# A graph network's tile loop in another order: four-batch tiles alternating with merged ones, SyncE's queue unrolled

## The reference, cut to what matters

```python
dst = (12500 * uniform(400000) ** 2).astype(int32); order = argsort(dst)
# layer 0: Gaussian mixture convolution, K = 3 kernels over edge attributes
gauss = exp(sum(-0.5 * (attr - mu)**2 / (eps + sigma**2)))
aggr  = segment_sum(einsum('eko,ek->eo', (x[src] @ g).reshape(E, 3, 64), gauss), dst) / max(cnt, 1)
x = layernorm(x + silu(aggr + x @ root_w + bias + x))
# layer 1: two mean-aggregating convolutions
h = relu(x @ W_self1 + (segment_sum(x[src], dst) / deg) @ W_neigh1 + b1)
x = layernorm(x + h @ W_self2 + (segment_sum(h[src], dst) / deg) @ W_neigh2 + b2)
```

## Time and profile before

| | us |
|---|---|
| median of 3 runs | 7653.07 |
| profiled execution | 7651.4 |
| its span | 7649.6 |
| TensorE busy | 5050.4 (66%) |
| VectorE busy | 4374.6 (57%) |
| GpSimd busy | 3367.5 (44%) |
| ScalarE busy | 2714.0 (35%) |

### The profile page before, as it was taken

How to read it: one execution, slowest core, us unless ns; L and a number is a source line. 1 busy time by engine, 2 the same in 40 slices (tenths; PEclk the granted TensorE clock), 3 DMA queues, 4 the chain that set the end, 5 groups by cost and what they waited for, 6 DMA issues and landing times.

```text
span 7649.6 us, 144672 instructions
## 1 busy us (share of the span) xinstructions
PE 5050.4 (66%) x35195; PEld 4048.2 (53%) x35196; DVE 4374.6 (57%) x15088; ACT 2714.0 (35%) x8317; POOL 3367.5 (44%) x3146
## 2 busy tenths in 40 slices
PE   1565655555566666655555555555545899999999
PEld 1223333333344444444444444444425899999999
DVE  5668888767677777665656656566543322222222
ACT  3113333334444444455555555555532000000000
POOL 5024555555666666666666666666630000000000
PEclk9558888877788888777778888788775899999999
DMA  2001222212222222222222222222230799999998
GB/s 71 28 24 49 68 68 68 67 51 87 78 96 83 87 91 90 90 90 91 90 90 91 91 90 90 73 90 90 91 85 3 298 381 383 381 367 385 385 384 344
DMA packets 258352, 1082.32 MB, mean 141 GB/s; under 512 B 140102, under 2 KB 144230, under 8 KB 194406
## 3 DMA queue, kind: packets, MB, share of 16 engines
q1 hardware_dynamic: 142806, 968.66, 32.8%
q0 software_dynamic: 100352, 102.96, 6.9%
q10 hardware_dynamic: 14902, 8.11, 0.5%
HBM read 751.67 MB, written 327.81 MB: 141 GB/s over the span
## 4 chain that ended last, share of the span: by engine, by line
PE 39%; DVE 20%; issue 14%; DVEq 13%; POOL 5%; DMA 5%; ACT 4%; ACTq 1%; SPq 1%; POOLq 0%
PE pw L970 21%; PE pw L800 9%; DVE rE L1269 5%; POOL rE L512 5%; DVEq L1302 3%; DMA tab<-tab_d 3%; DVEq L1472 3%; PE pw L825 3%; DVE rE L1267 2%; DVE rE L1329 2%; PE pw L772 2%; ACT rE L559 1%; DVE rE L1395 1%; PE pw L937 1%; ACT sca L575 1%
## 5 line engine op out<-in xcount | busy, mean ns | idle before, releaser
L512 POOL DMA_INDIRECT rE<-in_x,idx x3136 | 3365.4, 1073 | 2262.7 <-issue 2092.9
L800 PE MATMUL pw<-rE 128*128 128x193 f32 x7824 | 1775.9, 391 | 921.5 <-DVE rE L1329 885.9
L598 ACT CAST rB<-pw 128x792 bf16<-128x792 f32 x1568 | 1259.6, 814 | 2903.6 <-PE pw L825 1489.4
L800 PEld LDWEIGHTS pw<-rE 128*128 128x128 f32 x7824 | 1623.7, 233 | 1130.5 <-DVE rE L1329 1061.5
L559 ACT ACTIVATE rE<-rE,cols 128x64 f32<-128x64 f32 x4704 | 1254.5, 344 | 8.2 <-DMA tab<-tab_d 8.2
L825 PE MATMUL pw<-rE 128*128 128x396 f16 x3840 | 804.1, 357 | 577.8 <-DVE rE L1269 576.8
L1269 DVE TENSOR_SCALAR rE<-iperm,gr 128x392 f16<-128x392 f16 x3840 | 1052.1, 314 | 0.0
L825 PEld LDWEIGHTS pw<-rE 128*128 128x128 f16 x3840 | 368.8, 103 | 954.4 <-DVE rE L1269 681.1
L970 PE MATMUL pw<-rB,rA 128*128 128x192 bf16 x9604 | 810.8, 246 | 0.1
L970 PE MATMUL pw<-rE,rA 128*128 128x192 bf16 x9604 | 810.4, 246 | 0.1
L970 PEld LDWEIGHTS pw<-rB,rA 128*128 128x128 bf16 x9604 | 790.8, 98 | 1.6
(11 more groups left out here) (256 smaller groups left out, 2626.6 us busy)
## 6 DMA issues: line engine op xcount, KB each, us to landing
rA<-count SPq DMA_DIRECT2D x392, 1568.0 KB, 8.5
count<-rB SPq DMA_DIRECT2D x98, 3136.0 KB
rE<-in_x,idx POOLq DMA_INDIRECT x3136
cols<-cols_d SPq DMA_DIRECT2D x98, 64.0 KB
cols_d<-rA SPq DMA_DIRECT2D x3, 1568.0 KB, 5.2
rA<-in_edge_attr ACTq DMA_DIRECT2D x1, 4608.0 KB
out<-gcol ACTq DMA_DIRECT2D x97, 32.0 KB, 5.8
count<-rB SPq DMA_DIRECT2D x8, 224.0 KB, 2.0
```

The lines of the kernel that those rows point to most:

```text
L512: pool.indirect_dma_start(out=gath[:, s, u * CB + b, :], out_offset=None, in_=x, in_offset=bass.IndirectOffsetOnAxis(ap=idx[:, s, u * CB + ...
L598: act.copy(stage[:, s, :, j * 2 * W:(j + 1) * 2 * W].rearrange("p h (w n) -> p w h n", w=2), pu[j % 3][:, :, 0:CW].rearrange("p w (h n) -> ...
L800: ins = pe.matmul(sums[side][:, 0:AW], onehot[:, side, bb, :], wgath[:, side, bb, :], start=(bb == 0), stop=(bb == CB - 1))
```

## The change

Every engine goes through the tiles by position q instead of t. ORDER gives the tile of a position: 0, 1, 2; then 48, 3, 49, 4, ... 60, 15; then 61; then 16 to 47; then 62 to 97. NI = 13, QC = 30 is the first position of the two-batch tiles and QM = 62 that of the last merged ones. Semaphores count positions; which node tile is worked on, and which DRAM rows are read and written, comes from ORDER.

- TensorE, VectorE and ScalarE get a loop of 13 rounds whose body is a merged tile (always slot 1) followed by a four-batch tile (always slot 0).
- A four-batch tile now prepares the merge of the tile behind it. The merge works on a buffer of its own, `gm`.
- `merge_ahead` stands behind unit 6 instead of unit 4, and ScalarE's copies come one window later.
- A merged tile behind one of another kind (`behind=2`) waits for more used ring slots before its first units.
- SyncE's loops are written out: 98 times the same steps, with constant addresses, no registers.

```diff
+NI = T4 - DT - 1
+QC = DT + 2 + 2 * NI
+QM = QC + TM - T4
+ORDER = list(range(DT + 1)) + [t for i in range(NI) for t in (TM + i, DT + 1 + i)] + [TM + NI] \
+    + list(range(T4, TM)) + list(range(QM, 98))
...
+        gm = sb("gm", [P, LP])
...
-            for part, (base, n) in enumerate(PARTS):
-                end = part == len(PARTS) - 1
-                with sp.Fori(0, n // 2 - 2 * end, 1) as i:
-                    for s in range(2):
-                        after(part, i * 2 + s, s)
...
+            for q in range(NT):
+                part = max(k for k, (base, _) in enumerate(PARTS) if ORDER[q] >= base)
+                sp.wait_ge(a_evac, q * NU + (NU + 2))
+                sp.wait_ge(a_bnd, q + 1)
+                sp.dma_start(tile_of(count[part][0], ORDER[q] - PARTS[part][0]), stage[:, q % 2, None, 0:NT, :]).then_inc(a_st[q % 2], 16)
+                if q + 2 < NT:
+                    sp.wait_ge(a_list, q + 1)
+                    load_cols(q + 2)
+                if q + 3 < NT:
+                    for u in range(U):
+                        sp.wait_ge(a_g[1 - q % 2][u], 16 * CB * ((q + 1) // 2 + 1))
+                    load_idx(q + 3)
...
-                        if merged == "parts" and 6 <= j < 10:
-                            copied(i * 2 + (s + 1), 1 - s, j - 6)
+                        if merged == "parts" and 7 <= j < 11:
+                            copied(m, 1 - s, j - 7)
...
+            with act.Fori(0, NI, 1) as i:
+                windows(i + 1, 1)
+                windows(i + 2, 0, False, "parts", i + 1)
...
-                        dve.wait_ge(a_used, t * NU + (n + 1))
+                        free = n + 1 if behind < 2 else max(n + 1, min(n + 3, 4))
+                        dve.wait_ge(a_used, q * NU + free)
...
-                        if n == 4 and not last:
-                            merge_ahead(t + 1)
-                        if n == NU - 2 and not last:
-                            merge(t + 1)
...
+            def merge_between(n, q, following, other):
+                t, m = following
+                if n == 6:
+                    merge_ahead(q + 1, t, m, other)
+                if n == NU - 2:
+                    merge(m)
...
-            tile_counts(DT, 2, late=False)
-            with dve.Fori(0, T4 - DT - 1, 1) as i:
-                tile_counts(i + (DT + 1), 2)
...
+            tile_counts(DT, DT, 2, late=False, s=0, following=(TM, 0))
+            with dve.Fori(0, NI, 1) as i:
+                merged_counts(i * 2 + (DT + 1), i + TM, s=1)
+                tile_counts(i * 2 + (DT + 2), i + (DT + 1), 2, s=0, following=(i + (TM + 1), i + 1))
+            merged_counts(QC - 1, TM + NI, s=1)
+            with dve.Fori(0, QM - QC, 1) as i:
+                tile_counts(i + QC, i + T4, 1)
```

More of the change, by code:

```diff
@@ L384, in _ @@
             sp.sem_inc(a_col, 1)
-            for s in range(2):
-                load_cols(s, s)
+            for q in range(2):
+                load_cols(q)
             for u in range(U):
                 sp.wait_ge(a_g[0][u], 16 * CB)
[L389 to L409, removed]
+            load_idx(2)
             def tile_of(c, t):
@@ L574, in copied, with windows @@
                                             skip_runtime_bounds_check_because="the tables hold places of two columns")
-                    ins = act.copy(both[:, :, j], gr[:, bass.ds(at, 2)])
+                    ins = act.copy(both[:, :, j], gm[:, bass.ds(at, 2)])
                 if part is None or part == 3:
                     ins.then_inc(a_mrg, 1)
-            def windows(i, s, last, merged=None):
+            def windows(i, s, last=False, merged=None, m=None):
                 act.wait_ge(a_st[s], 16 * i + 1)
@@ L860, in listed, with tile_counts @@
                 pe.sem_inc(a_list, 1)
-            def tile_counts(t, pairs_w, late=True):
-                s = pe.snap(t % 2, min_val=0, max_val=1) if not isinstance(t, int) else t % 2
+            def tile_counts(t, pairs_w, late=True, s=None):
+                other = next_of(t) if s is None else 1 - s
+                s = pe.snap(t % 2, min_val=0, max_val=1) if s is None else s
                 for u in range(U):
@@ L871, in tile_counts @@
                         if late and n == 2 // max(1, pairs_w) - 1:
-                            listed(next_of(t) if not isinstance(t, int) else 1 - t % 2)
+                            listed(other)
                         if n % (NU // U) == 1:
@@ L1481, in tile_counts @@
                         if late and n == 2 // pairs_w - 1:
-                            listed(t - 1, slot_of(t + 1) if not isinstance(t, int) else 1 - t % 2)
-                            base_of(t)
+                            listed(q - 1, other)
+                            base_of(q, t)
                         if n % (NU // U) == 1:
-                            prepare(t, s, u)
+                            prepare(q, s, u)
+                        if following is not None:
+                            merge_between(n, q, following, other)
                 for k in range(2):
@@ L1495, in _ @@
             dve.sem_inc(a_pair, DT * NU)
-            tile_counts(DT, 2, late=False)
-            with dve.Fori(0, T4 - DT - 1, 1) as i:
-                tile_counts(i + (DT + 1), 2)
-            dve.wait_ge(a_used, T4 * NU + RU)
-            for _ in range(22):
-                dve.sem_inc(s_tick[3], 1)
-            with dve.Fori(0, TM - T4, 1) as i:
-                tile_counts(i + T4, 1)
-            dve.wait_ge(a_pair, TM * NU)
-            merge_ahead(TM)
-            merge(TM)
-            for _ in range(1):
-                dve.sem_inc(s_tick[3], 1)
-            with dve.Fori(0, NT - 1 - TM, 1) as i:
-                merged_counts(i + TM)
-            merged_counts(NT - 1, True)
+            tile_counts(DT, DT, 2, late=False, s=0, following=(TM, 0))
[5 more added lines that the diff above has]
+                tile_counts(i + QC, i + T4, 1)
+            dve.wait_ge(a_pair, QM * NU)
+            merge_ahead(QM, QM, QM - TM, 0)
+            merge(QM - TM)
+            with dve.Fori(0, NT - 1 - QM, 1) as i:
+                merged_counts(i + QM, i + QM, behind=1, following=(i + (QM + 1), i + (QM + 1 - TM)))
+            merged_counts(NT - 1, NT - 1, s=1, behind=1)
             listed(NT - 1, (NT - 1) % 2)
```

141 lines of the change are left out of this document (75 added, 66 removed).

## The result

| | us, median (lowest to highest), runs |
|---|---|
| before, beside the changed kernel | 7653.09, 4 runs |
| after | 7416.6 (7410.16 to 7425.55), 4 runs |
| ratio, 95% interval | 0.9692 (0.9675 to 0.9708) |
| profiled execution after | 7417.34, span 7415.5 |

The forecast was 7560 (7500 to 7635).

The account below looks back on a forecast made before the run. VectorE was taken to set the pace up to tile 48, GpSimd's gathers after that. Terms -72 (pairs), -15 (lead) and -5 (last tiles) sum to -92: 7651.4 to 7559, median 1.7 higher, 7560 us; range 7500 to 7635.

Parts of the forecast that it names:

- The pair: Alternating four-batch and merged tiles: VectorE's sum of 115.3 less 5.0 gives about 110 us a pair, -72 in all.
- each kind had both before: nothing: Table load L1302 at tile starts: fixing merged tiles to slot 1 and four-batch ones to slot 0 costs 0.
- The block repeats its 1640.9: Two-batch tiles 16 to 47 follow with buffers full as before, take 1640.9 us again, so 0 saved.
- the longest that two buffers allow: Lead (start of a tile's L1415 minus start of its first gather) at tile 16: 121 us, taken as the maximum.
- The -15 for the lead: Tile 62 begins with a lead of 39 us, not 24, so the last gather comes 15 us earlier.
- The -5 for merge_ahead: Merged tiles 62 to 97: later merge_ahead gives nothing while gathers bound; 5 of 12 us of tab waits go at the end.
- Gathers bound the pair: Rival, chance 0.08: in the alternating tiles the pair falls to 98 us, set by gathers; kernel 7410 us.
- The waits change hands: Rival, chance 0.08: vanished tab waits in merged tiles return as waits for TensorE and ScalarE; 7655 us, no change.
- Slower by instruction fetch: Rival, chance 0.10: VectorE's longer pair loop pays a fetch of 9.4 us per pair; kernel 7682 us.
- ScalarE's copies in four-batch tiles: 32 copies of 0.19 us a tile, covered by ScalarE's waits for TensorE: taken as 0, 51 us if uncovered.
- the stricter wait on the ring: First merged window pairs: VectorE waits for the last four-batch unit; taken as 0, bounded by 25 us in all.
- SyncE's queue: Unrolled queue sheds register work ahead of its issues: taken as 0, at best 5 us of the last tiles' tab waits.

Follow-up runs that it names:

- the order alone: Changed kernel with merge_ahead back behind window pair 4 and 64 increments ahead of VectorE's two-batch loop: 7514.96 us, ratio 0.9819.
- The two single edits: Changed kernel with merge_ahead and ScalarE's copies back early: 7473.82 us, ratio 0.9767; kernel before with both late: 7597.89 us, ratio 0.9932.

## Why the forecast was wrong

The forecast counted nearly all of its gain as one cause, the order, and gave the place of merge_ahead 5 us. There were three causes, and they add: 7652 - 7515 = 137 us for the order, 50 for the place of the two-batch loop, 57 for the place of merge_ahead (each of the last two alone; both together 7515 - 7417 = 98).

*The pair (term mis-sized, -72 forecast, -137 measured).* Mechanism and bound were right: a pair costs VectorE's sum, no DMA wait in it, ScalarE never short of gathers, GpSimd stalling. The pair took 104.7 us and not 110. VectorE's busy time is the same, 55.4 + 29.1 = 84.5 us in a four-batch tile and one of tiles 48 to 52 before, 1096.6 / 13 = 84.4 in a pair. So all is in the gaps, 11.7 + 18.6 = 30.3 before and 20.3 after. I took 5.0 off, and listed only the waits of the merged tiles for it: that is the step that failed. The largest wait stood in the other tile: 69.2 us by issue ahead of L1346, 5.3 a four-batch tile, of which 2.0 / 13 = 0.2 is left, now that this tile follows in straight code. (That straight code is the reason was tested only at the other head, where it took 2.0 of 7.0 away.) Against it stand 7.0 us a pair at the loop's new head (25.8 + 64.3 over 13) where a merged tile had 3.9 (19.5 in tiles 48 to 52), so 2.1 net. Part of that is a zero of the forecast that was none. The table load takes 4.7 us from slot 1 and 1.6 from slot 0, and "each kind had both before: nothing" overlooks that only the merged tile's load is still waited for, and that it now always comes from slot 1 (64.3 / 13 = 4.9 us a pair). With merged tiles in slot 0 it would be some 3.1 us a pair less, 40 in all; this is an estimate, no run tried it. The others, per pair: the table's DMA 4.5 (I had 3.5), the list's waits 4.6 to 3.2, and L1367 1.0, which I had at 0.6. L1249 did not fall, 4.8 to 5.1, where I had 0.9. These five give 8.7 of the 10.0. Neither constant slots nor the place of merge_ahead change the pair: 104.2 and 104.8 us with those taken back.

*"The block repeats its 1640.9" (step failed).* With the order alone it does, 1641.7, and tile 62 begins with a lead of 36 us, forecast 39. The step failed because it took the block's code to stay as it was. I had the fetch as a rival for the new loop and looked for it as a cost that the change adds. It was a cost that the old kernel paid, 3.0 us at each jump of the two-batch loop, and that the new program's length happened to remove. The rows named for it were those of the four-batch loop; the issue time of the two-batch loop (200.1 us) and the queue's 268 packets stood in the same trace and were not used. The lead at the start of the block was not the same either, 81 us and not 121: "the longest that two buffers allow" is no fixed number. GpSimd may start a tile some 12 us behind the mark two tiles back (above), so the longest lead is two tiles of that stage less 12.

The Trainium skill (Runtime: NRT & Kernel Launch, Instruction fetch mechanics) says that instructions stand in two 16 KiB pages and that a taken branch out of them stalls. The four packet counts and the 3.0 us above agree with such a stall. Which loop pays is not told by length alone: the same loop does so at one place and does not at another.

*The last stage (-15 and -5 forecast, -54 measured).* The -15 for the lead did not come: with the order alone the stage takes 1739.1 instead of 1740.2, and GpSimd needs 1731 us from tile 62's first gather to tile 97's instead of 1719. The -5 for merge_ahead was the term that failed most: "while gathers bound, that is nothing". The two single edits show 54 and 57 us. The lead of 22 to 24 us did say that gathers set the pace, but their pace is not fixed: it was 49.1 us a tile with the early place and 48.2 to 48.3 with the late one, and the issue of a gather is longer beside some of VectorE's work (below). And at the end, where the lead grows from 22 to 45, all of that growth was VectorE's own, and I granted 5 of it.

*The rivals.* "Gathers bound the pair" named 7410, and 7416.6 came, but that is a coincidence and not its mechanism: its mark was a pair of 98 us, and pairs are 104.7. "The waits change hands" did not happen in the pairs; in the last stage it did (L1455's wait for TensorE rose from 55 to 106 us when the table's went), and the time fell all the same. "Slower by instruction fetch" named a real cost, 2.0 us a pair at the new loop's head, but the larger fetch cost, that of the two-batch loop, went away.

*The zeros.* ScalarE's copies in four-batch tiles, the stricter wait on the ring and SyncE's queue cost nothing that shows: ScalarE still waits 417.0 us for TensorE there, the first window pairs of the merged tiles (L1395) wait 0.7 us for TensorE in all, and the unrolled queue alone has ratio 1.0000.

## What to carry to other kernels

An edit that makes a program longer moves every loop behind it, and whether a loop's jump back is fetched anew can change with that: look at the instruction queue's packets and at the issue time at each loop's head in the kernel before, and count it as something that can go as well as come. Padding that moves a loop also takes time itself: subtract it. A constant lead says who sets the pace, the gathers where it is short and the other engines where it is near two tiles. It does not say that the pace is fixed, so a wait of the other engine there is not free. When an edit fixes which buffer a tile uses, look whether the buffer matters to any instruction. And when waits are listed for a sum, list them for every tile in it, not for those alone whose wait has a name.

## What the runs showed of the hardware

GpSimd's issue of a gather is longer beside two of VectorE's instructions. Gathers of places 62 to 92 by what VectorE did during the issue (worked out from the start and end of each instruction in the traces; L1312 and L1329, in the changed kernel L1311 and L1328, are the 128x768 and 128x1024 f32 operations of layer 0, with two tiles as inputs):

| kernel | VectorE under 5% busy | beside L1312 or L1329 | beside other work only |
|---|---|---|---|
| before | 944 ns x303 | 1232 ns x351 | 982 ns x338 |
| merge_ahead early, changed kernel | 944 ns x298 | 1234 ns x343 | 982 ns x351 |
| after | 944 ns x316 | 1183 ns x353 | 984 ns x323 |
| merge_ahead late, kernel before | 944 ns x311 | 1154 ns x359 | 983 ns x322 |

Beside an idle VectorE it is 944 ns in all four, and nearly that beside most of VectorE's work: of 114 us over 944 ns a gather in the kernel before, 101 fall to the middle column. That column is shorter in the two kernels without the wait for the table, with as many gathers in it. Why it is shorter was not isolated.

The same load of VectorE's registers from the table takes 1.6 us from slot 0 and 4.7 from slot 1 in every kernel here, whichever kind of tile it belongs to.

VectorE's loop over two-batch tiles, some 340 instructions in the built program, paid 3.0 us more at each jump back in one place of the program than in another, 64 or 89 instructions away. Its loop over pairs, some 720 instructions, paid 2.0 us ahead of its first work, and nothing when written out.
